# Weighing eight heads in one piece, with eight pairs of exponentials held, in the sixteen-head attentions of a fused kernel

## The chip, the cores and the metric

The kernel runs on one core of one Trainium2 chip. The metric is the device time in microseconds of one execution; three runs of the kernel before gave a median of 2002.47 us (1995.29 to 2004.57).

## The reference, cut to what matters

The program is a chain of twelve sub-layers on a residual of 8 x 256 tokens by 128 features. Two of its kinds are attentions with sixteen heads of width 8: the causal one (`_L1_attn_ref`, once) and the two-expert one (inside `_L3_ffn_ref`, used twice; its two experts double the number of heads).

```python
# L1, causal, 8 batches of 256 tokens, 16 heads of 8
scores = jnp.einsum('bhqd,bhkd->bhqk', q, k) * scale
scores = jnp.where(causal, scores, jnp.finfo(scores.dtype).min)
attn = jax.nn.softmax(scores, axis=-1)
out = jnp.einsum('bhqk,bhkd->bhqd', attn, v)
...
# L3, not causal, m = 2 experts
scores = jnp.einsum('mbhtk,mbhsk->mbhts', q, kk) / jnp.sqrt(jnp.float32(KD))
attn = jax.nn.softmax(scores, axis=-1)
ctx = jnp.einsum('mbhts,mbhsk->mbthk', attn, v)
```

## The kernel before, in words

Both attentions are one class, `SmallHeads` (`L1Attend` and `L3Attend` derive from it). The work is cut into units: one unit is sixteen heads of one batch of 256 tokens. `L1Attend` has 8 units, `L3Attend` 16 (8 batches by 2 experts), and `L3Attend` runs twice in the program. The order of the work is written by hand: `steps()` counts steps s, sixteen to a unit (k is the unit, i the step in it), and each engine walks through the same steps and does what is due at each. There is no scheduler. The engines meet by semaphores, and each takes its instructions in order.

What TensorE (PE) does for a unit is spread over four units' worth of steps:

- Step (k, i): the scores of head i of unit k, two bf16 matmuls from 48 rows, into one of three PSUM banks (`score_bank`). A score waits until the reduction of three steps before has left its bank (`topped`). VectorE (DVE) takes the row maximum of each head (L1484 in L3; L1482, two instructions with a mask, in L1).
- i = 0: the projections of unit k+2 (`project`, 128x256 with w_L3m or w_L1a).
- i = 3: the split maxima of unit k-1 are turned (ident_b matmuls). They come from GpSimd (POOL, L1522 to L1528), which waits for the last maximum; ScalarE (ACT, L1437) copies them out, and a DMA puts them into the stacked operands as three more rows, so that the second pass has 51 rows.
- Each odd step: a pair of heads of the second pass (`pair_at`, LAG = 25 steps after the head's scores), now with the maximum subtracted, four bf16 matmuls, into two of three other banks (`shifted_bank`). A pair waits until the first exponential of the pair before it is done (`exped`, 2g - 1). ACT takes the two exponentials (L1455, 128x512 in L3, 128x384 in L1) and writes them into `self.pt[g % 4]`, four buffers of one pair each. In L1, POOL then clears the two diagonal blocks (L1515) and raises `selected`.
- A quad (`quad_at`): four heads are weighed with their values: fp32 matmuls of 128 rows by 18 columns, four side by side in the four column groups of the array, into bank 6. The order tool's rows write them as 18x256 x8 in L3 and 18x256 x4 with 18x128 x4 in L1. The quad waits for its four exponentials (in L1 for `selected`). Four quads make a unit. In L3 they fall on i = 14, 2, 6 and 10, in L1 on i = 0, 4, 8 and 12.
- With the fourth quad of a unit (i = 10 in L3, 12 in L1) ACT copies bank 6 (`raw`, L1461), waiting for `weighed`; it does so before it takes the next exponentials.
- i = 5: `raw` is turned (L1351); DVE takes the reciprocals (L1490) and scales (L1493), behind the maximum of head 5 in its queue. i = 7: the values of unit k (128x128 with wv), for which PE waits for `scaled`, since both use bank 7. ACT copies them (L2237 in L3, L1667 in L1). i = 9: the context is turned back (L1365), ACT copies it with the bias (L2242, L1671). i = 11: the output product (w_L3m or w_L1a, 128x256), in L3 only in every second unit.

`S.activation(self.pt[g % 4]...)` is L1455, the quads' matmuls are at L1409, but all of PE's products go through the helper `mm`, so the profile shows them at L195. The shapes tell them apart: 48*128 is a score, 51*128 a pair, 128*18 a quad. In a PE row of the trace such neighbours are merged under the first one's shape.

Of the kernel before, what the change touches and what calls it, by code (L numbers as in the profile page):

```python
# [10 lines left out]
ACT = mybir.ActivationFunctionType  # L11
AXX = mybir.AxisListType.X

P = 128
# [5 lines left out]
BANK = 512  # L20
# [4 lines left out]
DEPTH, L0_HEADS, L0_DIM, WINDOW = 2, 8, 64, 64  # L25
# [1180 lines left out]
class SmallHeads(Stage):  # L1206
# [11 lines left out]
    def __init__(self, k, name, group, tag, members, causal):  # L1218
        super().__init__(k, name)
        a = self.arena  # L1220
        self.group, self.tag, self.members, self.units, self.causal = group, tag, members, BATCH * members, causal
        self.h = a.take(TOKENS)
        self.whole = [a.take(TOKENS) for _ in range(self.STACKS)]
        self.buffer2 = self.whole[2:4]
        self.stacks = [t.bitcast(BF16).rearrange("p (x g s) -> p x g s", x=2, g=self.PAIRS) for t in self.whole]
        self.q, self.kk = [t[:, 0] for t in self.stacks], [t[:, 1] for t in self.stacks]
        self.qk = [a.take(2 * SEQ).rearrange("p (x s) -> p x s", x=2) for _ in range(2)]
        self.rest = a.take(2 * SEQ).rearrange("p (x s) -> p x s", x=2)
        self.parts = a.take_bf16(2 * PARTS * SEQ).rearrange("p (a s) -> p a s", a=2 * PARTS)
        self.masked = a.take_bf16(3 * 3 * P).rearrange("p (e s) -> p e s", e=3)  # L1230
        self.va = [a.take(2 * HEADS * 3 * (KD + 1)).rearrange("p (n d) -> p n d", n=2 * HEADS) for _ in range(3)]
        self.mx = [a.take(2 * HEADS).rearrange("p (t h) -> p t h", t=2) for _ in range(2)]
        self.mx_rest = a.take(2 * HEADS).rearrange("p (x g) -> p x g", x=4)
        self.mx_parts = [a.take_bf16(2 * PARTS * HEADS).rearrange("p (x a g) -> p x a g", x=4, a=PARTS) for _ in range(2)]
        self.mx_rows = [a.take_bf16(SEQ, PARTS * HEADS) for _ in range(2)]
        self.pt = [a.take(2 * BANK).rearrange("p (h c) -> p h c", h=2) for _ in range(4)]
        self.raw = a.take(BANK)
        self.rinv = a.take(2 * HEADS).rearrange("p (a j) -> p a j", j=2)
        self.ctx = a.take(2 * P)
        self.ctxT = [a.take(SEQ) for _ in range(2)]  # L1240
        self.scale = float(1.0 / np.sqrt(np.float32(KD)))
        self.n1 = P if causal else SEQ
        U, H = self.units, HEADS
        self.cleared, self.opened = self.sig("cleared", 1), self.sig("opened", 1)
        self.projected, self.biased, self.low = (self.sig(n, U) for n in ("projected", "biased", "low"))
        self.valued, self.v_copied = self.sig("valued", U), self.sig("v_copied", U)
        self.scored, self.topped = self.sig("scored", H * U), self.sig("topped", H * U)
        self.mx_split, self.mx_turned, self.mx_copied = (self.sig(n, U) for n in ("mx_split", "mx_turned", "mx_copied"))
        self.shifted, self.exped, self.selected = self.sig("shifted", H * U), self.sig("exped", H * U), self.sig("selected", self.PAIRS * U)
        self.weighed = self.sig("weighed", self.QUADS * U)  # L1250
        self.raw_copied, self.turned, self.scaled, self.turned_again, self.ctx_copied = (
            self.sig(n, U) for n in ("raw_copied", "turned", "scaled", "turned_again", "ctx_copied"))
        self.summed, self.added = self.sig("summed", BATCH), self.sig("added", BATCH)
        self.loads = 2 * len(RUNS)
        turns = [(U + self.STACKS - 1 - i) // self.STACKS for i in range(self.STACKS)]
        self.parts_out = [self.sig(f"parts_out{i}", 16 * n) for i, n in enumerate(turns)]
        self.stacked = [self.sig(f"stacked{i}", 16 * self.loads * n) for i, n in enumerate(turns)]
        self.mx_stacked = [self.sig(f"mx_stacked{i}", 32 * n) for i, n in enumerate(turns)]
# [8 lines left out]
        g = (s - self.LAG) // 2  # L1267
        return g if s % 2 and 0 <= g < self.PAIRS * self.units else None

    def quad_at(self, s):  # L1270

        s -= self.LAG + (7 if self.causal else 5)
        w = s // 4
        return w if s % 4 == 0 and 0 <= w < self.QUADS * self.units else None

    def norm_at(self, s, steps):

# [43 lines left out]
    def heads_tensor(self, eng):  # L1321
        k_, ps, mm, T, U = self.k, self.k.ps, self.k.mm, self.k.nc.tensor, self.units
        for s, k, i in self.steps():
# [58 lines left out]
            if g is not None:  # L1382
# [6 lines left out]
                for t, (st, cnt, at) in enumerate(((0, SEQ, 0), (SEQ - self.n1, self.n1, SEQ))):  # L1389
                    for e in range(2):  # L1390
                        rows = slice(64 * e, 64 * e + self.ROWS + PARTS)
                        o = mm(ps[:, self.shifted_bank(2 * g + e), at:at + cnt], kk[rows, x, t * P:(t + 1) * P], q[rows, x, st:st + cnt])
                        if t:
                            o.then_inc(self.shifted.sem, 1)
            w = self.quad_at(s)
            if w is not None:
                u, x = w // self.QUADS, w % self.QUADS
                self.wait_ge(eng, *((self.selected, 2 * w + 2) if self.causal else (self.exped, 4 * w + 4)))
                if w == 0:
                    self.wait_ge(eng, self.opened, 1)  # L1400
                if x == 0:
                    self.wait_ge(eng, self.v_copied, u + 1)
                    self.wait_ge(eng, self.raw_copied, u)
                c, j = x // 2, x % 2
                for t, (st, cnt, at) in enumerate(((0, SEQ, 0), (SEQ - self.n1, self.n1, SEQ))):
                    for f in range(4):
                        h = 4 * x + f
                        v = self.va[u % 3][:, t * HEADS + h, (KD + 1) * (1 - j):(KD + 1) * (3 - j)]
                        o = mm(ps[32 * f:32 * f + 2 * (KD + 1), 6, c * SEQ + st:c * SEQ + st + cnt], v,  # L1409
                               self.pt[(2 * w + f // 2) % 4][:, f % 2, at:at + cnt], start=j == 0 and t == 0, stop=j == 1 and t == 1)  # L1410
                o.then_inc(self.weighed.sem, 1)
            c = self.norm_at(s, self.NORM_CENTERS)
            if c is not None:
# [9 lines left out]
    def heads_scalar(self, eng):  # L1423
        k_, ps, S = self.k, self.k.ps, self.k.nc.scalar
        for s, k, i in self.steps():
# [23 lines left out]
            g = self.pair_at(s)  # L1449
            if g is not None:  # L1450
                both = SEQ + self.n1
                self.wait_ge(eng, self.weighed, (g - 4) // 2 + 1)
                for e in range(2):
                    self.wait_ge(eng, self.shifted, 2 * g + e + 1)
                    S.activation(self.pt[g % 4][:, e, 0:both], ps[:, self.shifted_bank(2 * g + e), 0:both], ACT.Exp, scale=self.scale).then_inc(self.exped.sem, 1)  # L1455
            w = self.quad_at(s)
            if w is not None and w % self.QUADS == self.QUADS - 1:
                u = w // self.QUADS
                self.wait_ge(eng, self.weighed, w + 1)
                self.wait_ge(eng, self.turned, u)  # L1460
                S.activation(self.raw, ps[:, 6, :], ACT.Copy).then_inc(self.raw_copied.sem, 1)  # L1461
# [46 lines left out]
    def heads_gpsimd(self, eng, ch):  # L1508
        G, U = self.k.nc.gpsimd, self.units
        for s, k, i in self.steps():  # L1510
            g = self.pair_at(s)
            if self.causal and g is not None:
                pt = self.pt[g % 4][:, :, 0:3 * P].rearrange("p h (b c) -> p h b c", b=3)[:, :, 0:3:2]
                self.wait_ge(eng, self.exped, 2 * g + 2)
                G.affine_select(pt, pt, [[0, 2], [0, 2], [1, P]], ALU.is_ge, 0.0, base=0, channel_multiplier=-1).then_inc(self.selected.sem, 1)  # L1515
            u = k - 1
# [1136 lines left out]
```

## Time and profile before

| | |
|---|---|
| median of 3 runs | 2002.47 us (1995.29 to 2004.57) |
| span of the profiled execution (the page gives no other time of it) | 2003.0 us |
| TensorE busy | 84% |
| VectorE busy | 65% |
| ScalarE busy | 58% |
| GpSimd busy | 29% |
| the chain that ended last | PE 62%, DVE 13%, ACT 11%, issue 7%, POOL 4%, DMA 2% |
| causal attention (L1), from its first to its last score's maximum | 997.0 to 1099.7 us |
| the two L3 attentions, first to last maximum | 1354.9 to 1924.2 us, with experts and a scan between them |

The span is the time from the first to the last instruction of the profiled execution. Busy shares are means over the whole program, whose stages have different limits, so they don't say what bounds the attentions. A PE row of the timeline gives the start of a group, its length up to the modelled end of its last matmul, and in brackets what ended the idle time ahead of it. In the chain of waits each piece is the work that the next one waited for.

### The profile page before, as it was taken

What the parts mean: (1) busy time and instruction counts of PE and PEld (TensorE: products, weight loads), DVE (VectorE), ACT (ScalarE), POOL (GpSimd) and SP (SyncE); (2) the same over time, 40 slices, a digit from 0 to 9 for tenths busy, and PEclk for the clock granted to TensorE, in tenths of its full rate; (3) what the DMA queues carried; (4) which work ended last, traced back from release to release, by engine and by line L of the source; (5) the groups of instructions that cost most, each with busy time, mean ns of one, the idle gap of its engine ahead of it and who ended that gap; (6) DMA issues with size and microseconds to landing.
All of it is one profiled execution on the core that took longest, in us unless ns stands there. A gap on an engine that the chain in (4) does not pass through costs nothing.

```text
span 2003.0 us, 36848 instructions
## 1 busy us (share of the span) xinstructions
PE 1685.2 (84%) x13664; PEld 884.9 (44%) x13664; DVE 1299.4 (65%) x2611; ACT 1153.5 (58%) x2711; POOL 579.3 (29%) x727
## 2 busy tenths in 40 slices
PE   6897889798898889889688884978999877899986
PEld 2555345543455435553244332324555352355535
DVE  4875577545776577744577277637788464788856
ACT  3665455544455546555356664564888735488872
POOL 2552145301554045410265103313232001333200
PEclk9999999999899999989879897996999988699997
DMA  4000000000000000000252000015544000544401
GB/s 183 17 18 7 1 17 17 12 1 1 17 12 17 1 11 18 17 1 0 46 105 52 1 1 0 0 25 101 101 94 85 17 28 16 109 97 91 94 3 63
DMA packets 55016, 75.01 MB, mean 37 GB/s; under 512 B 5748, under 2 KB 38740, under 8 KB 54328
## 3 DMA queue, kind: packets, MB, share of 16 engines
q1 hardware_dynamic: 54840, 72.66, 16.0%
q8 instruction: 111, 1.82, 0.4%
q14 instruction: 65, 0.53, 0.1%
HBM read 46.39 MB, written 16.88 MB: 32 GB/s over the span
## 4 chain that ended last, share of the span: by engine, by line
PE 62%; DVE 13%; ACT 11%; issue 7%; POOL 4%; DMA 2%; SPq 0%; DVEq 0%; POOLq 0%; ACTq 0%
PE ps L195 58%; ACT arena L631 4%; DVE arena L1484 3%; PE ps L521 2%; ACT arena L1455 2%; DVE arena L702 2%; DVE arena L746 2%; ACT arena L268 1%; ACT arena L270 1%; PE ps L616 1%; PE ps L1365 1%; DVE arena L1493 1%; DMA arena<-arena 1%; DVE arena L721 1%; DMA arena<-scratch 1%
## 5 line engine op out<-in xcount | busy, mean ns | idle before, releaser
L195 PE MATMUL ps<-arena 32*64 32x128 f32 (+10 forms) x10152 | 705.0, 316 | 88.7 <-ACT arena L1455 25.5
L195 PEld LDWEIGHTS ps<-arena 32*64 32x64 f32 (+6 forms) x10152 | 397.7, 127 | 390.3 <-issue 124.5
L1455 ACT ACTIVATE arena<-ps 128x512 f32<-128x512 f32 (+1 forms) x640 | 333.8, 576 | 79.2 <-PE ps L195 70.4
L1484 DVE TENSOR_REDUCE arena<-ps 128x2 f32<-128x512 f32 x512 | 322.6, 685 | 87.2 <-PE ps L195 85.3
L195 PE MATMUL ps<-arena,w_L0f 128*128 128x512 f32 (+3 forms) x800 | 328.2, 542 | 16.9 <-DVEq L2488 9.3
L631 ACT ACTIVATE arena<-ps,arena 128x128 f32<-128x128 f32 x512 | 226.2, 460 | 136.0 <-DVE arena L748 136.0
L195 PE MATMUL ps<-arena,const 128*128 128x512 f32 (+1 forms) x536 | 186.1, 653 | 70.9 <-DVE arena L1966 22.1
L195 PEld LDWEIGHTS ps<-arena,w_L0f 128*128 128x128 f32 (+2 forms) x800 | 142.0, 192 | 142.4 <-issue 102.8
L828 POOL TENSOR_TENSOR arena<-arena 128x512 f32<-128x512 f32 x128 | 133.0, 1045 | 244.4 <-DVE arena L726 244.4
L702 DVE TENSOR_TENSOR arena<-ps,arena 128x1024 f32<-128x1024 f32 x128 | 152.4, 1205 | 10.0 <-PE ps L195 7.3
L642 ACT ACTIVATE arena<-ps 128x512 f32<-128x512 f32 x128 | 76.8, 600 | 94.4 <-DVE arena L702 91.7
L195 PEld LDWEIGHTS ps<-arena,const 128*128 128x128 f32 (+1 forms) x536 | 59.0, 161 | 158.2 <-issue 89.8
L820 POOL TENSOR_TENSOR arena<-arena 128x512 f32<-128x512 f32 x64 | 81.4, 1271 | 160.2 <-DVE arena L702 157.2
L746 DVE TENSOR_REDUCE arena<-ps 128x8 f32<-128x1024 f32 x64 | 78.3, 1223 | 63.7 <-PE ps L195 63.4
L721 DVE COPY arena<-ps 128x512 f32<-128x512 f32 x128 | 88.3, 689 | 47.7 <-PE ps L521 47.7
L631 ACT ACTIVATION_READ_ACCUMULATOR arena<-ps,arena 128x1 f32 x512 | 106.5, 208 | 0.0
L521 PE MATMUL ps<-const,arena 128*128 128x128 f32 x512 | 79.1, 277 | 30.2 <-issue 23.2
L1482 DVE CUSTOM_DVE_ANT_0 arena<-ps,masks_b 128x128 bf16<-128x128 f32 (+1 forms) x256 | 75.0, 354 | 36.2 <-PE ps L195 35.8
L521 PEld LDWEIGHTS ps<-const,arena 128*128 128x128 f32 x512 | 57.1, 141 | 93.2 <-issue 91.3
L1522 POOL CAST arena<-arena 128x32 bf16<-128x32 f32 x40 | 8.4, 209 | 280.0 <-DVE arena L1484 275.7
L821 POOL TENSOR_TENSOR arena<-arena 128x512 f32<-128x512 f32 x64 | 83.5, 1305 | 0.0
L195 PE MATMUL ps<-residual,const 128*128 128x512 f32 x96 | 56.9, 694 | 31.4 <-DVEq L2488 17.9
(227 smaller groups left out, 2134.2 us busy)
## 6 DMA issues: line engine op xcount, KB each, us to landing
scratch<-arena SPq DMA_DIRECT2D x40, 384.0 KB, 2.8
arena<-scratch SPq DMA_DIRECT2D x80, 192.0 KB
arena<-scratch SPq DMA_DIRECT2D x80, 128.0 KB
arena<-arena SPq DMA_DIRECT2D x64, 128.0 KB, 2.3
arena<-scratch SPq DMA_DIRECT2D x80, 88.0 KB
arena<-in_experts SPq DMA_DIRECT2D x16, 256.0 KB, 4.4
w_L0f<-in_L0f SPq DMA_DIRECT2D x2, 1557.0 KB, 12.2
arena<-arena SPq DMA_DIRECT2D x80, 12.0 KB
```

The source lines that it names most:

```text
L195: return self.nc.tensor.matmul(o, lhsT, rhs, start=start, stop=stop, skip_group_check=True)
L521: o = k.nc.tensor.transpose(k.ps[:, 6, (2 * j + t) * P:(2 * j + t + 1) * P], self.prob[G % 2][:, 2 * p + j, t, :], k.K("ident"))
L631: o = S.activation(self.prob[G % 2][:, j, t, :], k.ps[:, j, t * P:(t + 1) * P], ACT.Exp, bias=self.negm[G % 2][:, at:at + 1], scale=rn[:, ...
L642: self.k.nc.scalar.activation(self.sq[i], self.k.ps[:, self.block_bank(n), :], ACT.Square).then_inc(self.squared.sem, 1)
L702: self.k.nc.vector.tensor_tensor(prod.rearrange("p t (b s) -> p t b s", b=PER), x, tab, ALU.mult).then_inc(self.rotated.sem, 1)
L721: self.k.nc.vector.tensor_copy(self.probT[q % 4].rearrange("p j t s -> p (j t s)"), self.k.ps[:, 6, :]).then_inc(self.turn_copied.sem, 1)
L746: ch.did(V.tensor_reduce(self.mx[G % 2], ps[:, 0:4, 0:SEQ].rearrange("p j (t s) -> p j t s", t=2), AXX, ALU.max))
L820: G.tensor_tensor(y[:, i, :], first[:, 0, :], second[:, 1, :], ALU.add).then_inc(self.placed.sem, 1)
L821: G.tensor_tensor(y[:, i + 1, :], second[:, 0, :], first[:, 1, :], ALU.add).then_inc(self.placed.sem, 1)
L828: self.k.nc.gpsimd.tensor_tensor(pr, pr, rinv, ALU.mult).then_inc(self.scaled.sem, 1)
L1455: S.activation(self.pt[g % 4][:, e, 0:both], ps[:, self.shifted_bank(2 * g + e), 0:both], ACT.Exp, scale=self.scale).then_inc(self.exped.s ...
L1484: o = V.tensor_reduce(mx, ps[:, self.score_bank(s), :].rearrange("p (t s) -> p t s", t=2), AXX, ALU.max)
```

## The change

- Eight pairs of exponentials are held in place of four. The second four lie in the weights of the first sub-layer's local attention (`w_L0f0` and `w_L0f1`, two buffers of 1024 columns in each), which nobody reads any more when the attentions run. The index is `g % 8`, and ACT's wait for the quad that last read the buffer moves from four pairs back to eight.
- `quad_at` becomes `quads_at`: at every eighth step two quads are weighed one behind the other, in place of one at every fourth. In L3 they fall on i = 2 (quads 0 and 1) and i = 10 (quads 2 and 3), in L1 on i = 4 and i = 12. The second quad of each two keeps its step, the first comes four steps later than before. The copy of bank 6 stays at its step.
- Numbers of instructions, shapes and all other steps stay the same. The instructions of DVE and SP are in the same order as before.

```diff
-        self.pt = [a.take(2 * BANK).rearrange("p (h c) -> p h c", h=2) for _ in range(4)]
+        spent = [k.wt[f"L0f{l}"][:, x * 2 * BANK:(x + 1) * 2 * BANK] for l in range(DEPTH) for x in range(2)]
+        self.pt = [t.rearrange("p (h c) -> p h c", h=2) for t in [a.take(2 * BANK) for _ in range(4)] + spent]
...
-    def quad_at(self, s):
+    def quads_at(self, s):
 
-        s -= self.LAG + (7 if self.causal else 5)
+        s -= self.LAG + (11 if self.causal else 9)
         w = s // 4
-        return w if s % 4 == 0 and 0 <= w < self.QUADS * self.units else None
+        return (w, w + 1) if s % 8 == 0 and 0 <= w < self.QUADS * self.units else ()
...
-            w = self.quad_at(s)
-            if w is not None:
+            for w in self.quads_at(s):
...
                         o = mm(ps[32 * f:32 * f + 2 * (KD + 1), 6, c * SEQ + st:c * SEQ + st + cnt], v,
-                               self.pt[(2 * w + f // 2) % 4][:, f % 2, at:at + cnt], start=j == 0 and t == 0, stop=j == 1 and t == 1)
+                               self.pt[(2 * w + f // 2) % 8][:, f % 2, at:at + cnt], start=j == 0 and t == 0, stop=j == 1 and t == 1)
...
-                self.wait_ge(eng, self.weighed, (g - 4) // 2 + 1)
+                self.wait_ge(eng, self.weighed, (g - 8) // 2 + 1)
...
-                    S.activation(self.pt[g % 4][:, e, 0:both], ps[:, self.shifted_bank(2 * g + e), 0:both], ACT.Exp, scale=self.scale).then_inc(self.exped.sem, 1)
-            w = self.quad_at(s)
-            if w is not None and w % self.QUADS == self.QUADS - 1:
+                    S.activation(self.pt[g % 8][:, e, 0:both], ps[:, self.shifted_bank(2 * g + e), 0:both], ACT.Exp, scale=self.scale).then_inc(self.exped.sem, 1)
+            w = max(self.quads_at(s), default=0)
+            if w % self.QUADS == self.QUADS - 1:
...
-                pt = self.pt[g % 4][:, :, 0:3 * P].rearrange("p h (b c) -> p h b c", b=3)[:, :, 0:3:2]
+                pt = self.pt[g % 8][:, :, 0:3 * P].rearrange("p h (b c) -> p h b c", b=3)[:, :, 0:3:2]
```

PE in L3, from the pair and scores ahead of i = 14 to the quad of i = 10, before (18x256 is a quad, w_L3m 128x256 the projection of i = 0, ident_b i = 3, L1351 i = 5, w_L3m 128x128 i = 7, L1365 i = 9; 128x256 of the arena are scores and pairs):

```order
L195 MATMUL ps<-arena 18x256 x8
L195 MATMUL ps<-arena 128x256 x6
L195 MATMUL ps<-arena,w_L3m 128x256 x2
L195 MATMUL ps<-arena 128x256 x10
L195 MATMUL ps<-arena 18x256 x8
L195 MATMUL ps<-ident_b,arena 48x128 x2
L195 MATMUL ps<-arena 128x256 x8
L1351 MATMUL ps<-const,arena 128x128 x4
L195 MATMUL ps<-arena 128x256 x8
L195 MATMUL ps<-arena 18x256 x8
L195 MATMUL ps<-w_L3m,arena 128x128 x2
```

The same stretch of PE in the changed kernel:

```order
L195 MATMUL ps<-arena 128x256 x22
L195 MATMUL ps<-arena,w_L3m 128x256 x2
L195 MATMUL ps<-arena 128x256 x10
L195 MATMUL ps<-arena 18x256 x16
L195 MATMUL ps<-ident_b,arena 48x128 x2
L195 MATMUL ps<-arena 128x256 x8
L1352 MATMUL ps<-const,arena 128x128 x4
L195 MATMUL ps<-arena 128x256 x8
L195 MATMUL ps<-w_L3m,arena 128x128 x2
```

The quad of i = 14 has gone from between the scores to i = 2, and that of i = 6, between L1351 and the values, has gone to i = 10, outside the rows shown.

PE in L1 between i = 3 and i = 7 in the changed kernel, where one 18x256 x4 with its 18x128 x4 stood before:

```order
L195 MATMUL ps<-ident_b,arena 48x128 x2
L195 MATMUL ps<-arena 128x128
L195 MATMUL ps<-arena 128x256 x3
L195 MATMUL ps<-arena 128x128 x3
L195 MATMUL ps<-arena 128x256
L195 MATMUL ps<-arena 18x256 x4
L195 MATMUL ps<-arena 18x128 x4
L195 MATMUL ps<-arena 18x256 x4
L195 MATMUL ps<-arena 18x128 x4
L1352 MATMUL ps<-const,arena 128x128 x4
```

Quad 0, that stood at i = 0, now runs here ahead of quad 1 and of the turning of `raw` (L1352).

## Rows read from the trace of the kernel before

**Rows 1.** Stages by windows: us, busy time (instructions) by engine, PEclk, DMA share
```profile
1400.00:1500.00 100.00, 93.23 (x1083) 50.49 (x1079) 80.70 (x138) 81.53 (x164) 32.44 (x58) 1.00 0.46 94
...
1030.00:1090.00 60.00, 48.45 (x675) 26.92 (x674) 48.23 (x313) 41.82 (x99) 38.41 (x70) 1.00 0.39 79
...
1090.00:1120.00 30.00, 25.61 (x240) 11.44 (x242) 9.16 (x50) 17.03 (x40) 11.05 (x20) 0.71 0.01 2
```

**Rows 2.** The chain of waits in L3, pair of i = 13 to the next
```profile
1447.77 5.51 PE ps L195 x63
...
1453.31 1.18 DVE arena L1484 x2
...
1456.06 1.23 PE ps L195 x12
...
1460.89 5.51 PE ps L195 x63
```

**Rows 3.** PE's timeline in L3, in narrow windows: start us, us, group
```profile
1461.43 0.63 PE L195 MATMUL ps<-arena 128*18 128x256 f32 x8
...
1462.09 0.62 PE L195 MATMUL ps<-arena 128*18 128x256 f32 x6
...
1462.96 1.13 PE L195 MATMUL ps<-arena,w_L3m 128*128 128x256 f32 x4
...
1465.77 0.29 PE L195 MATMUL ps<-ident_b,arena 128*48 128x128 bf16 x2
...
1469.18 0.68 PE L195 MATMUL ps<-w_L3m,arena 128*128 128x128 f32 x4 [0.33 <-DVE arena L1493]
...
1472.66 1.13 PE L195 MATMUL ps<-arena,w_L3m 128*128 128x256 f32 x4
...
1474.98 0.28 PE L195 MATMUL ps<-arena 51*128 51x256 bf16 x2 [0.43 <-ACT arena L1455]
```

**Rows 4.** PE's weight loads in L3, the first behind a quad
```profile
1462.42 0.12 PEld L195 LDWEIGHTS ps<-arena 48*128 48x128 bf16 x4 [0.42 <-issue]
```

**Rows 5.** ACT's timeline in L3: the first exponential of i = 13
```profile
1461.38 0.60 ACT L1455 ACTIVATE arena<-ps 128x512 f32<-128x512 f32 x1
```

**Rows 6.** DVE's timeline in L3 around the scaling
```profile
1464.45 3.87 DVE L1484 TENSOR_REDUCE arena<-ps 128x2 f32<-128x512 f32 x6 [0.91 <-PE ps L195]
...
1468.61 0.42 DVE L1493 TENSOR_TENSOR arena<-ps,arena 128x256 f32<-128x256 f32 x1
```

**Rows 7.** The chain of waits in L3's tail
```profile
1583.80 1.09 ACT arena L1455 x2
...
1586.41 1.09 ACT arena L1455 x2
```

**Rows 8.** The chain of waits in L1, one unit
```profile
1052.15 1.90 PE ps L195 x26
...
1054.98 1.15 PE ps L195 x9
...
1057.46 0.88 ACT arena L1455 x2
...
1058.39 0.64 POOL arena L1515
...
1061.15 1.60 PE ps L195 x25
...
1065.16 0.84 PE ps L195 x5
```

**Rows 9.** L1: a quad on PE, and the first weight load behind it
```profile
1056.05 0.62 PE L195 MATMUL ps<-arena 128*18 128x256 f32 x7
...
1056.83 0.28 PEld L195 LDWEIGHTS ps<-arena 48*128 48x128 bf16 x8 [0.21 <-DVE arena L1482]
```

**Rows 10.** ACT's timeline in L1: exponentials of i = 7, copy of the context
```profile
1053.32 0.87 ACT L1455 ACTIVATE arena<-ps 128x384 f32<-128x384 f32 x2
...
1054.46 0.47 ACT L1671 ACTIVATE arena<-ps,cols 128x256 f32<-128x256 f32 x1 [0.26 <-PE ps L1365]
```

## The prediction

> **What bounds the kernel now.** I looked first at the stages, since only the three sixteen-head attentions can change. In the steady part of L3 (the second L3 attention reads the same) PE is busy for 93 of 100 us at a granted clock of 1.00, DVE and ACT for 81 each; in L1 PE and DVE have 48 of 60 us each, POOL 38 [rows 1]. A busy PE is a modelled figure, so the chain of waits decides. In L3 it repeats exactly [rows 2]. From the pair of i = 13 (1447.77, next 1460.89) PE itself is the chain for 5.51 us. Then DVE, with the maxima of heads 3 to 5 and the scaling, is the chain from 1453.31 until PE starts the values of i = 7 at 1456.06. From there it is PE again, up to the pair of i = 11, whose exponential on ACT releases the next pair of i = 13. The unit shown is one without an output product and takes 1460.89 - 1447.77 = 13.12 us. The next, with one, takes 1474.98 - 1460.89 = 14.09 us [rows 3]. The mean is 13.6 us.
>
> That difference of 0.97 us is the most useful number here: it is what one more block of work on PE behind the quad of i = 10 costs, and it is about what the product takes there (1472.66 to the next group, four passes of 0.22 us and a change of shape). Work added on PE at i = 10 or 11 therefore goes into the time one for one.
>
> **What a quad costs.** In L3 a quad is 16 matmul records, four side by side, so four waves. The first starts at 1461.43, the last at 1462.09 [rows 3], which makes 0.22 us from wave to wave. The next group's weights load at 1462.42 [rows 4]. From last wave to next group are 0.33 us, 0.11 more than a wave: the price of leaving this shape. No row prices the entering by itself; between nothing and the same again I take the same, about 0.10 for each change. The second of two quads behind each other thus adds 4 x 0.216 = 0.87 us and no change.
>
> **The change in a steady L3 unit, place by place.**
>
> 1. i = 10 gets quad 2 in addition: +0.87 us, one for one, as the output product shows. ACT can't help: it waits there for the end of both quads to copy bank 6.
> 2. i = 2 gets quad 0 in addition: +0.87 us. It lies in the stretch from 1460.89 to i = 3 at 1465.77 that is PE's own [rows 2, 3].
> 3. i = 14 loses its quad. PE's stretch from the pair of i = 13 (1460.89) to the projection (1462.96) is 2.07 us now [rows 3]. Without the quad PE comes to the pair of i = 15 after some 0.7 us, but this pair waits for the first exponential of i = 13: it starts on ACT at 1461.38 and takes 0.60 [rows 5], and PE goes on some 0.05 later, 1.15 us after 1460.89. The pair itself and the change of shape take 0.31 to the projection, so the stretch becomes 1.46 us: -0.61, not the whole 1.07 of a quad with its two changes. This wait is new and takes the quad's place.
> 4. i = 6 loses its quad: 0. Its 0.87 us lie under the DVE chain: from i = 3 (1465.77) to the values (1469.18) are 3.41 us, of which PE only needs the first two thirds. PE waits for L1493, which runs from 1468.61 to 1469.03 and stands behind the maximum of head 5 [rows 3, 6]. With the quad gone PE just waits about 1 us longer. The three maxima can't start earlier either, since head 3 comes from PE behind i = 3.
>
> The sum is 0.87 + 0.87 - 0.61 + 0 = **+1.13 us per unit**, 8% of 13.6. Two cheap blocks under cover are exchanged for two on the chain. DVE starves longer at i = 2, which costs nothing more, since PE's own time up to i = 3 is already counted.
>
> The 8 buffers by themselves cost and gain nothing. The old wait of ACT (a quad three steps back) always lay behind a pair that PE issues after that quad, so it was never last. The quads wait for exponentials of three steps ago as before. Where the buffers lie changes no instruction. The DMAs keep their place, and SP's order is the same.
>
> Of a stage's 16 units, 14 are steady (k = 2 to 15): +15.8 us. At k = 1 the quad of i = 14 goes away alone: -0.6. In the tail (k = 16, 17) pairs run without scores, at 2.61 us per four steps [rows 7], 1.09 of it the exponentials of a pair. With two quads between two pairs that gap becomes 2.15 us and the other three stay near 1.2, together 5.8 in place of 5.2 for eight steps: three times +0.55 = +1.6. An L3 stage has +16.8, both **+33.6 us**.
>
> **L1.** A unit takes 1065.16 - 1052.15 = 13.01 us. The chain [rows 8] goes from the values (1052.15) over PE to the output product (1054.98), the quad of i = 12, the copy of bank 6 and the exponentials of i = 13 and 15 (1057.46), two clearings on POOL (from 1058.39), the splitting of the maxima, i = 3 on PE (1061.15), the turning of `raw` and DVE's scaling to the next values. A quad is shorter: 1056.05 to 1056.83 with both changes [rows 9], 0.65 for a second one behind the first.
>
> - i = 8 loses its quad: the copy of the context, that started at 1054.46, then only waits for the exponentials of i = 7, which end at 1053.32 + 0.87 = 1054.19 [rows 10]: -0.27.
> - i = 12 gains one: +0.65. Up to i = 3 together +0.38: ACT's copy, the exponentials and both clearings are late by that much.
> - i = 0 loses its quad: 0, PE waits for POOL at i = 3 anyway.
> - i = 4 gains one, ahead of the turning of `raw`: +0.65.
>
> That is **+1.03 us per unit**, for six steady units +6.2. In the tail the granted clock is 0.71 in the mean [rows 1], so part of it at the lower level of 1.2 GHz, where a quad takes twice as long; I put +1.5 for it. L1 together: **+7.7 us**.
>
> **The sum**: 33.6 + 7.7 = +41.3 us on the profiled execution's span of 2003.0, which is the median (2002.47) to within 0.6 us. Forecast: **2044 us**, slower by 2.1%.
>
> **A rule that speaks for the change.** Each leaving of the 18-column shape shows as 0.11 us on PE [rows 3, 4]. The Trainium skill, "TensorEngine Tiling (Array Packing)", section "Key Properties", states that changing the tiling mode, not just the tile, drains the engine. By that rule alone, fewer changes of mode are fewer drains, and the kernel gets faster. The trace agrees that a change costs something, but the sum of the chain is not the sum of the drains.
>
> **The rivals.**
>
> - **Fewer changes of shape decide (faster).** If PE's own work bound every step, only the changes would count. A unit has three fewer: two around i = 14, and one of the three around i = 6, as the values still need their own. For 40 units, 3 x 0.10 x 40 = 12 us less: 1991 us. It would decide if PE's waits at i = 7 and i = 15 were not there. For it speaks PE's 93%. Against it: DVE's rows stand in the chain in every unit, and PE shows an idle time released by L1493 [rows 2, 3, 6]. Chance 0.07.
> - **The slack takes it all.** DVE and ACT are at 81%, so in principle 19% of a unit could absorb two longer blocks, and the deeper buffers could let them run ahead. Time 1999 to 2008. Against it: the three score banks and three pair banks are what limits running ahead, not the held exponentials, and the output product's 0.97 us are not absorbed either. Chance 0.05.
> - **Half of it.** If the pair of i = 15 isn't held up and i = 14 gives back its whole 1.07 us, a unit costs 0.87 + 0.87 - 1.07 = +0.67; with L1 at half its sum and no tail, 28 x 0.67 + 3 = +22: 2025 us. Chance 0.15.
> - **The clock goes too.** PE would idle some 1.5 us longer at a stretch in each unit, and where it had less to do around L1's tail the granted clock fell (0.71) [rows 1]. L1's steady part has 48 of 60 us busy and keeps 1.00, which speaks against it. If a tenth of the 540 us of attentions ran at 1.2 GHz, with PE on two thirds of the chain, that is some 25 us on top: 2069. Chance 0.08.
> - **The forecast**: 0.65.
>
> **The numbers.** The range goes from the half case to a starved case in which the double quads also make ACT late by another 0.3 us per unit (+12): 2021 to 2057. What lies outside are the faster and the unchanged case and most of the clock case, less than 2 in 10. A measurement of this kernel can tell about 0.5% (10 us) from no change. Slower by more than that: 0.88; within it, the slack case and the weak half of the first rival, 0.07; faster, 0.05.
>
> **What would show it.** If I am right, in L3 the unit with a product takes 15.2 us and the one without 14.25 in the chain; PE waits over 1 us for L1493 at i = 7; the pair of i = 15 is released by L1455 1.15 us behind the pair of i = 13; two quads take 1.73 us plus their changes, and the steady busy share of PE falls from 93% to about 87%. DVE idles about 1 us between heads 2 and 3. In L1 the unit takes about 14.0 us. I am wrong if the unit stays at 13.6 or less, if the values of i = 7 start earlier behind i = 3 than 3.4 us (then the scaling wasn't last there), or if PE shows other shapes' gaps shrinking.

## The result, and the profile after

The changed kernel takes 2074.31 us (median of 4 runs, 2069.11 to 2085.4) against 2000.11 for the kernel before. The ratio of the runs is 1.0367, with a 95% interval of 1.0329 to 1.0405: slower by 74 us, where the forecast said 41 and the range ended at 2057. The profiled execution has a span of 2083.7 us, 80.7 more than that of before; it is the slowest of the four, so the differences read from its trace are some 10 us larger than those of the medians.

First the chain of waits of one L3 unit without an output product, from values to values (start us, us, what):

```profile
1420.94 1.23 PE ps L195 x12
...
1422.71 3.20 PE ps L195 x47
...
1426.56 0.44 PE ps L195 x4
...
1427.05 0.61 ACT arena L1455
...
1427.70 4.62 PE ps L195 x55
...
1432.35 1.18 DVE arena L1484 x2
...
1433.55 0.68 DVE arena L1484
...
1435.10 1.23 PE ps L195 x12
```

The unit takes 1435.10 - 1420.94 = 14.16 us, where the forecast said 14.25; its counterpart in [rows 2] took 13.12, which was the longest of its kind: the other full units without a product in that trace take 13.04 or 13.05, so 13.04 + 1.13 = 14.17 was the figure to expect. The pair of i = 15 (1427.70) comes 1.14 us behind that of i = 13 (1426.56) and is released by the exponential in between (forecast 1.15). DVE is still the chain from head 3 to the scaling. PE's timeline of the same unit shows the wait that grew (start us, us, group, idle time ahead of it and its releaser):

```profile
1426.56 0.89 PE L195 MATMUL ps<-arena 51*128 51x256 bf16 x8 [0.45 <-ACT arena L1455]
1427.70 0.39 PE L195 MATMUL ps<-arena 51*128 51x256 bf16 x4 [0.25 <-ACT arena L1455]
...
1431.69 0.29 PE L195 MATMUL ps<-ident_b,arena 128*48 128x128 bf16 x2
...
1435.10 0.68 PE L195 MATMUL ps<-w_L3m,arena 128*128 128x128 f32 x4 [1.31 <-DVE arena L1493]
```

From i = 3 to the values are 3.41 us, as before [rows 3]; PE's wait there went from 0.33 to 1.31 us. A clean unit with an output product takes 15.20 us (forecast 15.2). Up to here the working holds. The rest is in the windows: us, busy time by engine, then the granted clock (PEclk). Two consecutive units, and the same stages as [rows 1]:

```profile
1420.94:1435.10 14.16, 12.02 (x144) 6.67 (x145) 10.63 (x19) 10.95 (x22) 4.46 (x8) 1.00 0.46 92
1435.10:1451.93 16.83, 14.66 (x149) 7.77 (x149) 11.07 (x20) 11.05 (x22) 4.39 (x8) 0.90 0.40 73
```
```profile
1400.00:1500.00 100.00, 86.45 (x934) 46.01 (x932) 68.45 (x118) 70.65 (x142) 31.08 (x56) 0.92 0.41 80
1800.00:1900.00 100.00, 86.80 (x926) 47.06 (x930) 69.37 (x119) 70.91 (x142) 28.14 (x54) 0.91 0.42 82
1030.00:1090.00 60.00, 48.04 (x562) 27.03 (x562) 38.95 (x254) 34.47 (x81) 33.24 (x59) 0.83 0.39 79
```

The second unit should take 15.20 and takes 16.83: part of it ran at the lower of the two clock levels (1.2 GHz), which makes a mean of 0.90, and costs 1.63 us. "Low stretch" below means such a time at the lower level. The two L3 attentions together have 24 intervals from one scaling to the next in which scores are still made. Before, none of them had a granted clock under 1.00, and neither had L1's first four; now 16 of the 24 have, and all four of L1's. PE's busy time per 100 us of L3 is 86.5, as forecast (87), though some of it is work at half speed; the clean unit above has 12.02 of 14.16 us, 85%.

By stages, in the profiled execution of each kernel (each stage from its first scaling to its last; in brackets the part of it at the lower clock level, us):

| run | L1 | both L3 attentions | all the rest |
|---|---|---|---|
| kernel before | 89.4 (23.9) | 383.8 (0) | 1529.9 |
| single_eight | 84.3 (6.8) | 383.6 (0) | 1528.2 |
| changed kernel | 104.7 (44.4) | 444.9 (71.7) | 1534.1 |
| fill_gap | 90.7 (6.8) | 421.0 (10.2) | 1532.6 |
| fill_other | 94.6 (17.1) | 454.7 (64.9) | 1530.5 |
| pair_first | 91.9 (17.1) | 398.2 (13.7) | 1533.5 |
| pair_second | 99.2 (41.0) | 427.6 (54.6) | 1527.7 |
| long_wait | 102.2 (51.2) | 407.0 (51.2) | 1528.7 |
| less_two | 84.2 (6.8) | 373.8 (17.1) | 1526.2 |
| less_two_warm | 85.6 (10.2) | 371.2 (10.2) | 1522.2 |

The 89.4 us of L1 in the kernel before are unusual: single_eight, less_work, less_at_10, less_two, less_all and less_two_warm leave L1's instructions as they were and have 84.2 to 86.9. What differs is the tail, where the trace that the forecast was read from had more of the lower clock than the others.

### The profile page after: what moved, and what is told of

Its sections match the earlier page's. It is cut to its first block, busy times and chain, and to the rows that moved or that the text cites. A ratio compares the mean times of both kernels' runs of the same rounds, so it can differ in the third digit from the quotient of the medians.

```text
span 2083.7 us, 36836 instructions
## 1 busy us (share of the span) xinstructions
PE 1727.2 (83%) x13664; PEld 908.3 (44%) x13664; DVE 1298.1 (62%) x2611; ACT 1154.3 (55%) x2711; POOL 579.7 (28%) x727
## 4 chain that ended last, share of the span: by engine, by line
PE 63%; DVE 14%; ACT 11%; issue 7%; POOL 3%; DMA 2%; SPq 0%; DVEq 0%; POOLq 0%; ACTq 0%
PE ps L195 58%; ACT arena L631 4%; DVE arena L1484 3%; PE ps L521 2%; ACT arena L1455 2%; DVE arena L702 2%; DVE arena L746 1%; ACT arena L268 1%; ACT arena L270 1%; PE ps L616 1%; PE ps L1366 1%; DVE arena L721 1%; DMA arena<-arena 1%; DMA arena<-scratch 1%; DVE arena L1493 1%
## 5 line engine op out<-in xcount | busy, mean ns | idle before, releaser
L195 PE MATMUL ps<-arena 32*64 32x128 f32 (+10 forms) x8872 | 647.1, 314 | 100.7 <-ACT arena L1455 27.6
L195 PEld LDWEIGHTS ps<-arena 32*64 32x64 f32 (+6 forms) x8872 | 378.0, 132 | 376.5 <-issue 133.1
L195 PE MATMUL ps<-arena,const 128*128 128x512 f32 (+1 forms) x536 | 191.6, 672 | 68.9 <-DVE arena L1966 22.1
L828 POOL TENSOR_TENSOR arena<-arena 128x512 f32<-128x512 f32 x128 | 133.2, 1047 | 240.9 <-DVE arena L726 240.9
L1455 ACT ACTIVATE arena<-ps 128x512 f32<-128x512 f32 (+1 forms) x320 | 167.1, 576 | 35.5 <-PE ps L195 30.7
L1455 ACT ACTIVATE w_L0f<-ps 128x512 f32<-128x512 f32 (+1 forms) x320 | 166.8, 574 | 35.3 <-PE ps L195 28.7
L195 PE MATMUL ps<-w_L0f,arena 128*18 128x256 f32 (+2 forms) x1408 | 168.9, 476 | 0.0
L820 POOL TENSOR_TENSOR arena<-arena 128x512 f32<-128x512 f32 x64 | 81.4, 1272 | 162.4 <-DVE arena L702 159.5
L521 PEld LDWEIGHTS ps<-const,arena 128*128 128x128 f32 x512 | 57.1, 141 | 92.7 <-issue 90.7
## 6 DMA issues: line engine op xcount, KB each, us to landing
w_L0f<-in_L0f SPq DMA_DIRECT2D x2, 1557.0 KB, 12.3
```

The source lines that it names most:

```text
L195: return self.nc.tensor.matmul(o, lhsT, rhs, start=start, stop=stop, skip_group_check=True)
L521: o = k.nc.tensor.transpose(k.ps[:, 6, (2 * j + t) * P:(2 * j + t + 1) * P], self.prob[G % 2][:, 2 * p + j, t, :], k.K("ident"))
L820: G.tensor_tensor(y[:, i, :], first[:, 0, :], second[:, 1, :], ALU.add).then_inc(self.placed.sem, 1)
L828: self.k.nc.gpsimd.tensor_tensor(pr, pr, rinv, ALU.mult).then_inc(self.scaled.sem, 1)
L1455: S.activation(self.pt[g % 8][:, e, 0:both], ps[:, self.shifted_bank(2 * g + e), 0:both], ACT.Exp, scale=self.scale).then_inc(self.exped.s ...
```

## The experiments

The runs are described below. Full-clock unit times are the distance from one scaling to the next in units whose granted clock is 1.00 throughout, without and with an output product. PEclk is the granted clock of 1400 to 1560 us, which lies inside the first L3 attention in each kernel. It says nothing of the second L3 attention or of L1. The kernel before has 13.04 and 14.09 us and 1.00. Each ratio is taken against the kernel before run beside it, whose median was 1996.94 to 2003.18 us, so a few us between medians of different runs mean nothing.

| run | median us | ratio (95%) | L3 unit at full clock | PE's wait at i = 7 | PEclk |
|---|---|---|---|---|---|
| changed kernel | 2074.31 | 1.037 (1.033 to 1.041) | 14.16 / 15.20 | 1.31 | 0.90 |
| single_eight | 1996.67 | 0.998 (0.995 to 1.001) | 13.04 / 14.08 | 0.33 | 1.00 |
| fill_gap | 2045.16 | 1.022 (1.016 to 1.027) | 14.16 / 15.20 | 0.33 | 0.99 |
| fill_other | 2087.73 | 1.047 (1.042 to 1.051) | 14.77 / 15.81 | 1.31 | 0.95 |
| pair_first | 2022.40 | 1.010 (1.004 to 1.016) | 13.29 / 14.34 | 0.33 | 0.99 |
| pair_second | 2054.81 | 1.026 (1.019 to 1.032) | 13.91 / 14.95 | 1.32 | 0.91 |
| pairs_shifted | 2043.58 | 1.023 (1.018 to 1.028) | 13.59 / 14.28 | none | 0.97 |
| less_work | 1997.36 | 1.001 (0.999 to 1.003) | 13.04 / 14.09 | 0.98 | 0.99 |
| long_wait | 2046.01 | 1.023 (1.019 to 1.028) | 13.27 / 14.30 | 1.31 | 0.96 |
| less_at_10 | 2004.97 | 1.002 (1.000 to 1.005) | 12.97 / 13.43 | 0.33 | 0.94 |
| less_all | 2024.63 | 1.012 (1.005 to 1.019) | 12.17 / 12.64 | 1.17 | 0.78 |
| less_two | 1994.95 | 0.998 (0.996 to 1.001) | 12.78 / 13.25 | 0.54 | 0.98 |
| less_two_warm | 1981.93 | 0.991 (0.987 to 0.994) | 12.78 / 13.25 | 0.55 | 0.98 |

### single_eight: the buffers alone

```diff
     def quads_at(self, s):
-        s -= self.LAG + (11 if self.causal else 9)
+        s -= self.LAG + (7 if self.causal else 5)
         w = s // 4
-        return (w, w + 1) if s % 8 == 0 and 0 <= w < self.QUADS * self.units else ()
+        return (w,) if s % 4 == 0 and 0 <= w < self.QUADS * self.units else ()
```

> The changed kernel with its eight buffers, but with single quads at their old steps. Both theories (the places of the quads cost the time, with or without the clock) expect the time of before, 2000 us within 0.3%, and L3 units of 13.04 and 14.09 us. If the buffers or their place in the spent weights cost something, the time stays above 2010.

0.998: no difference, and the same units as before. Eight buffers, four of them in the spent weights, cost and gain nothing. All of the 74 us come from where the quads stand.

### fill_gap and fill_other: the same added work at two places

```diff
+            for w in self.filler_at(s):
...
+                        mm(ps[32 * f:32 * f + 2 * (KD + 1), 6, c * SEQ + st:c * SEQ + st + cnt], v,
+                           self.pt[(2 * w + f // 2) % 8][:, f % 2, at:at + cnt], start=t == 0, stop=t == 1)
             for w in self.quads_at(s):
```

`filler_at` (cut here) gives quad 2 in L3 (i = 6) and quad 0 in L1 (i = 0), at the steps of before. The real quads overwrite what the filler writes.

> The changed kernel with its double quads, and one more quad in addition whose result is thrown away (bank 6 is overwritten by the real one): in L3 at i = 6, where PE otherwise waits 1.3 us for the scaling, in L1 at i = 0, where it waits for POOL. Clock theory: the low granted clock in the changed kernel comes from these waits of PE; with them filled the clock stays at 1.00 in the steady part, the added work is free, L3 units take 14.2 and 15.2 us each, and the whole takes 2040 to 2045 us, some 30 us less than without the added work. Rival (the double blocks, or something else about the new order, lower the clock or delay the engines): the time stays at 2074 or rises by the added work.

The kernel with the work of a quad more per unit takes 29 us less than without it: 2045.16. PE's timeline of fill_gap in L3, from the double quad of i = 10 to the values:

```profile
1448.59 1.92 PE L195 MATMUL ps<-w_L0f,arena 128*18 128x256 f32 x32
1450.44 1.13 PE L195 MATMUL ps<-arena,w_L3m 128*128 128x256 f32 x4
...
1459.92 1.06 PE L195 MATMUL ps<-w_L0f,arena 128*18 128x256 f32 x16
1461.30 0.68 PE L195 MATMUL ps<-w_L3m,arena 128*128 128x128 f32 x4 [0.33 <-DVE arena L1514]
```

The releaser, L1514 in this kernel's numbering, is the same scaling (L1493 before). The wait is back at 0.33 us, the added quad (1459.92) lies fully under it, and the units at full clock are unchanged, 14.16 and 15.20. So the work was free and what it brought is the clock:

```profile
1400.00:1560.00 160.00, 146.78 (x1744) 79.78 (x1746) 117.79 (x202) 119.35 (x238) 46.06 (x85) 0.99 0.44 88
```

for which the changed kernel has

```profile
1400.00:1560.00 160.00, 139.17 (x1472) 74.00 (x1474) 108.19 (x185) 111.57 (x224) 45.43 (x85) 0.90 0.41 82
```

fill_gap also has both double quads, so these don't lower the clock by themselves. Its profiled span is 2044.3 us, 41.3 more than before. That this is just the sum of the forecast is in part luck: against single_eight, whose L1 tail is the usual one, the L3 attentions take 37.4 us more (forecast 33.6; three low stretches are in it), L1 6.5 (forecast 7.7) and the rest of the program 4.4 (forecast 0).

> As fill_gap, with the same quad's worth of added work in L3, but at i = 14, where PE has only some 0.4 us of waiting, in place of i = 6; the wait of 1.3 us at i = 7 stays. If that long wait is what lowers the clock: low stretches stay in the steady L3 units and the work added on the chain (about 0.6 us a unit) comes on top: 2075 to 2100 us. If the clock only goes by how much PE does in a unit (rival): no low stretches, units of 14.8 and 15.9 us, 2062 us.

fill_other puts its L3 filler at quad 0's old step, i = 14, with everything else the same. The units at full clock grow by 0.61 as forecast (14.77 and 15.81), the low clock stays, and the time is 2087.73. PE's wait at i = 7 is the changed kernel's:

```profile
1441.12 0.68 PE L195 MATMUL ps<-w_L3m,arena 128*128 128x128 f32 x4 [1.31 <-DVE arena L1514]
```

The same amount of added work brings 29 us at one place and costs 13 at another. In 1400 to 1560 us the clock is better than in the changed kernel (0.95 against 0.90), but over both L3 attentions it is nearly the same: 64.9 us at the lower level, against 71.7 there and 10.2 in fill_gap. So the place decides, and that the amount counts too isn't shown. L1 has the filler at i = 0 in both runs, and in both it is shorter than in the changed kernel (90.7 and 94.6 against 104.7 us).

### pair_first and pair_second: one double quad each

```diff
     def quads_at(self, s):
-        s -= self.LAG + (11 if self.causal else 9)
+        s -= self.LAG + (7 if self.causal else 5)
         w = s // 4
-        return (w, w + 1) if s % 8 == 0 and 0 <= w < self.QUADS * self.units else ()
+        if s % 4 or not 0 <= w < self.QUADS * self.units:
+            return ()
+        x = w % self.QUADS
+        return {1: (w - 1, w), 2: (w,), 3: (w,)}.get(x, ())
```

(pair_second has `{0: (w,), 1: (w,), 3: (w - 1, w)}`.)

> Only quads 0 and 1 of each unit are weighed together (i = 2 in L3, i = 4 in L1); quads 2 and 3 keep their steps. By the chain of waits a steady L3 unit costs 0.87 - 0.61 = +0.26 us and an L1 unit +0.65: 7 + 4 = +11 us, 2011. Clock theory: the wait for the scaling at i = 7 stays at 0.3 to 0.4 us, so no steady L3 unit shows a low granted clock, and 2011 is all. Rival (double blocks or the new wait at i = 15 lower the clock): low stretches in steady L3 units, at 1.6 us each, 2020 or more.

> Only quads 2 and 3 are weighed together (i = 10 in L3, i = 12 in L1); quads 0 and 1 keep their steps. By the chain alone a steady L3 unit costs +0.87 us, an L1 unit +0.4: 24 + 2 = 2027 us. Clock theory: PE's wait at i = 7 grows to 1.3 us as in the changed kernel, steady L3 units show low stretches, and the time is 2045 to 2060. Rival (it isn't that wait): 2027 and a clock of 1.00 in the steady units.

The chain's terms come out to 0.01 us: pair_first has 13.29 and 14.34, +0.25 (forecast +0.26); pair_second 13.91 and 14.95, +0.87 (forecast +0.87). The sum of both is the changed kernel's +1.12. In L3 the clock falls widely only with the second (0.91 against 0.99), the one that empties i = 6. The totals are higher than the chain's: pair_first is at 2022, not 2011, and so where the expectation had put the rival. Two low stretches at the end of each L3 attention cost about 3 us there, 6 in both. L1 takes 7.6 us more than in single_eight, where some 4 were expected, and has 17.1 us at the lower level against 6.8. In pair_second L1 has 41.0 us at the lower level, although its quad at i = 0 keeps its place: there i = 8 is emptied.

### less_work and long_wait: the wait without the double quads

less_work is the kernel before with quad 2 of L3 multiplied from truncated operands:

```diff
                         v = self.va[u % 3][:, t * HEADS + h, (KD + 1) * (1 - j):(KD + 1) * (3 - j)]
+                        pt = self.pt[(2 * w + f // 2) % 4][:, f % 2, at:at + cnt]
+                        if x == 2 and not self.causal:
+                            v, pt = v.bitcast(BF16)[:, 1::2], pt.bitcast(BF16)[:, 1::2]
...
```

long_wait is pair_second with the same three lines.

> The kernel before, with one thing less for PE: in L3, quad 2 (i = 6, under the scaling) is multiplied from the upper halves of its fp32 operands, read as bf16, so heads 8 to 11 are weighed with truncated numbers. That takes about 0.65 us of PE's work out of every L3 unit, at the one place that the chain of waits doesn't use; PE's wait at i = 7 grows from 0.33 to about 1 us. Clock theory: some steady L3 units get a low granted clock, at 1.6 us each, and the kernel becomes slower though it does less: 2005 to 2030 us. Chain alone (rival): L3 units stay at 13.04 and 14.09 us with a clock of 1.00, 2000 us.

> As pair_second (quads 2 and 3 together at i = 10 in L3, 12 in L1), with L3's quad 2 multiplied from the upper halves of its operands, read as bf16, as in less_work. PE has the same work in an L3 unit as in less_work, but its wait for the scaling at i = 7 is 1.3 us in place of 0.98, and the chain is some 0.2 to 0.3 us longer. If the length of the wait decides on the clock: low stretches in a third to a half of the steady L3 units, 2025 to 2040 us. If only the amount of PE's work counts (rival): steady L3 units as clean as in less_work, 13.3 and 14.4 us, and about 2018 us (of which some 12 are L1's, as in pair_second).

PE's wait in less_work and in long_wait:

```profile
1448.74 0.68 PE L195 MATMUL ps<-w_L3m,arena 128*128 128x128 f32 x4 [0.98 <-DVE arena L1495]
```
```profile
1446.51 0.68 PE L195 MATMUL ps<-w_L3m,arena 128*128 128x128 f32 x4 [1.31 <-DVE arena L1498]
```

less_work was a miss: with a wait of 0.98 us its steady L3 units are 13.04 and 14.09, one of the 24 intervals touched by the low clock, and the time is that of before. The other half of it is confirmed: 0.65 us of work out of i = 6 shortens the unit by nothing. long_wait, with the same work per L3 unit and a wait of 1.31 us, has low stretches in 11 of the 24 and takes 2046, 28 us more than the 2018 without low stretches in L3, and more than the 2025 to 2040 expected. In its trace the L3 attentions take 23 us more than in single_eight, of which the chain explains some 6, and L1 18 us more. Between the two kernels lie a third of a microsecond of waiting at i = 7 and quad 2 at i = 10 in place of i = 6, and in L1 a quad moved too. So the same work in an L3 unit can keep the clock or lose it. That the wait does it fits fill_gap, but these two runs don't separate it from the order around it, and there is no simple length: L1 before had a wait of 1.38 us in each unit and kept 1.00 [rows 1], as the trace of before shows at 1052.15:

```profile
1052.15 0.68 PE L195 MATMUL ps<-w_L1a,arena 128*128 128x128 f32 x4 [1.38 <-DVE arena L1493]
```

### pairs_shifted: both double quads under cover

```diff
-        s -= self.LAG + (11 if self.causal else 9)
+        s -= self.LAG + (15 if self.causal else 13)
```

> The changed kernel with both double quads four steps later: L3 at i = 6 and i = 14, L1 at i = 8 and i = 0. By the chain, L3's double quad at i = 6 is mostly under the scaling (+0.5 us, the half us that PE comes late to the values), i = 10 gives back 0.4 to 0.75, i = 14 takes 0.87 and i = 2 gives 0.95 back: a unit of 13.0 and 13.7 us, 13.4 in the mean against 13.6 before. L1: +0.35 at i = 0, -0.7 at i = 4, +0.65 at i = 8, -0.75 at i = 12: 12.5 us. The clock theory expects 1.00 in the steady L3 units, since PE doesn't wait at i = 7 any more. Together 1990 to 1995 us, a little faster than before. If double blocks hurt by themselves: slower than before, 2010 or more.

A miss. The units are 13.59 and 14.28 us, 0.6 more than I had worked out, and the end of each L3 attention is longer, since the last double quad waits at i = 14. Nor does the clock stay at 1.00, as the clock theory had it: though PE doesn't wait at i = 7 any more, 41 of 421 us in L3 are at the lower level, most of them at the end of each attention. The chain shows what I left out (start us, us, what):

```profile
1482.69 0.42 issue
1483.12 0.59 ACT w_L0f L1455
1483.71 0.37 ACT arena L2242
...
1484.12 1.69 PE ps L195 x11
1485.81 0.59 ACT arena L1455
```

The double quad at i = 6 makes the pair of i = 7 late, and through it ACT: its exponentials and the copy of the context (L2242) become the chain up to the output product.

### less_at_10, less_all, less_two, less_two_warm: less work, and the version that beats both

These are less_work's edit with other quads of L3: `x == 3`; all four; `x % 2` (quads 1 and 3). less_two_warm adds to less_two:

```diff
-                for t in range(2):
+                for t in (0, 0, 0, 1) if i == 13 and not self.causal and k >= 2 else (0, 1):
```

> The kernel before, with quad 3 of L3 (i = 10) in place of quad 2 multiplied from the upper halves of its operands, read as bf16: the same 0.65 us of work less for PE as in less_work, but at a place where I hold that work counts one for one. A unit with an output product should come down by 0.65 to 13.4 us; one without by about 0.3 to 12.7, since the pair of i = 11 then waits for an exponential. 28 steady units: 1983 to 1988 us. Rival (the sum of PE's work counts, not the place): as less_work, where the same saving gave nothing, 1997.

> The kernel before, with all quads of L3 multiplied from the upper halves of their operands, read as bf16 (all heads of L3 weighed with truncated numbers), in their old places. By the chain: i = 2 gives 0.65 us, i = 10 0.3 to 0.65, i = 14 the 0.4 us up to the wait for the exponential, i = 6 nothing: about 1.5 us a unit, 12.1 in the mean, 1958 us if the clock holds. PE is then idle for over 2 us a unit, among it 1 us at i = 7. Clock theory: low stretches come and take back part of it, 1965 to 1995 us.

> The kernel before, with quads 1 and 3 of L3 (i = 2 and i = 10, the two places on PE's own chain) multiplied from the upper halves of their operands, read as bf16 (heads 4 to 7 and 12 to 15 of L3 weighed with truncated numbers), and quads 0 and 2 (i = 14 and 6, which lie beside waits) left in fp32. Chain at full clock: i = 2 gives 0.65 us, i = 10 0.1 to 0.65: units of 12.3 and 12.8 us, 33 us less in 28 units. Clock theory: PE's busy stretches at i = 6 and 14 are kept, so there is less of the low clock than in less_all, but some, as in less_at_10: 1970 to 1995 us. It would be the first version faster than both kernels. If total work decides: as less_all, 2015 or more.

> As less_two, with added work for PE in L3: the first of the two products of head 13's score is issued three times (the same numbers into the same place), just ahead of PE's wait for the exponential at i = 13. The chain pays nothing in units without an output product and up to 0.2 us in the others. If more work beside the wait keeps the clock up: fewer low stretches than in less_two and some 5 to 10 us less. If two bf16 products more don't matter to the clock: the same as less_two within 3 us, or up to 4 us more.

At i = 10 the work counts where an output product follows (14.09 to 13.43, forecast 13.4), and hardly without one (12.97, forecast 12.7). In the chain of such a unit the exponential at i = 11 comes next. But steady units get the low clock, and the time, 2004.97, is not below that of before: a miss of 17 us. less_all, a miss too (1965 to 1995 expected), shows it at its plainest. Its window:

```profile
1400.00:1560.00 160.00, 141.47 (x1268) 74.46 (x1266) 121.24 (x206) 121.35 (x244) 45.21 (x84) 0.78 0.44 87
```

PE has 2.6 us of work less in each unit, a clean unit takes 12.17 or 12.64 us (12.4 in the mean, forecast 12.1), and the kernel is slower than before, 2024.63 against 2001.08, because half of L3 (208 of 411 us) runs at the low level. PE's waits in a unit of it:

```profile
1450.44 0.68 PE L195 MATMUL ps<-w_L3m,arena 128*128 128x128 f32 x4 [1.17 <-DVE arena L1495]
...
1455.27 1.53 PE L195 MATMUL ps<-arena 51*128 51x256 bf16 x20 [0.85 <-ACT arena L1457]
```

less_two keeps the covered quads in fp32. Its units are 12.78 and 13.25 us, not the 12.3 and 12.8 forecast: beside less_at_10 the work taken from i = 2 brings 0.2 us and not 0.65, as DVE's maxima become the chain there (in the chain of waits of less_two at i = 2 and 3; before they came in only at head 3):

```profile
1444.71 2.84 DVE arena L1486 x5
```

The clock is 0.98. Its ten runs spread from 1982.98 to 2007.70 (median 1994.95), so it can't be told from before. less_two_warm adds two products of head 13's score that change nothing just ahead of the wait at i = 13, which become part of that wait:

```profile
1454.07 2.14 PE L195 MATMUL ps<-arena 51*128 51x256 bf16 x28 [0.85 <-ACT arena L1457]
```
```profile
1447.33 2.14 PE L195 MATMUL ps<-arena 51*128 51x256 bf16 x28 [0.64 <-ACT arena L1457]
```

(first less_two, then less_two_warm). The units are the same to 0.01 us, and the time is 1981.93 (1974.61 to 1987.00): ratio 0.991, 0.987 to 0.994. It is faster than both kernels by about 1%, with products that nobody needs, and with heads 4 to 7 and 12 to 15 of L3 weighed with truncated numbers. Against less_two the medians are 13 us apart. The two profiled executions are only 5.2 us apart, half of it in the L3 attentions, with 10.2 us at the lower level against 17.1, and the window of the table has 0.98 in both. So the added products made it faster, but that they did so through the clock is shown only in small part.

## Why the prediction was wrong

**What held.** Every term of the chain of the forecast in L3 at full clock. One block at i = 10: +0.87, measured +0.87 alone. The two moves around i = 2 and i = 14: +0.26, measured +0.25. The quad of i = 6 under the scaling: 0, measured 0 by less_work and by fill_gap. The sum +1.13, measured +1.12. L1's block at i = 4 was +0.65 and measured 0.56 (13.57 against 13.01 in a clean unit of pair_first); clean L1 units of fill_gap take 13.8 to 14.2 against a forecast of 14.04. With most of the clock held, the whole was 2045.16 against a forecast of 2044, in part by luck, as said at fill_gap.

**What failed** is first of all the term of 0 at i = 6 in L3 ("i = 6 loses its quad: 0", with "PE just waits about 1 us longer"). On the chain of waits 0 is right. For the time it is not, because the forecast held the clock at 1.00. The quad at i = 6 was PE's work in its longest wait of the L3 unit. With the work put back there and at i = 0 in L1, 29 us come back (changed kernel against fill_gap); without it they stand on top of the chain's 41. L1's terms, too, were priced on the chain alone. The rival "The clock goes too" named this mechanism, at a chance of 0.08 and with its 2069 us outside the range. The reason given against it, that L1's steady part has 48 of 60 us busy and keeps 1.00, was no reason. PE's busy share doesn't decide it: the changed L3 is busy for 86 of 100 us, more than L1 was, and has 0.92. The rival's own size was low too, a tenth of the attentions at the lower level: in the changed kernel it is 116 of 550 us. Against fill_gap this is 99 us more, and the traces are 39 us apart: 24 in the two L3 attentions, 14 in L1 and 1 or 2 elsewhere. So a third of the loss is L1's, whose steady part went from 1.00 to 0.83, and one us at the lower level cost about 0.4 us in either.

The rival on fewer changes of shape wasn't borne out: the kernel got slower, and every term of the chain is matched without it. The slack rival and the half case fell with the +1.12. The tail's +1.5 us in L1 was worked out from a tail with more of the lower clock than the other kernels show, so no run confirms it.

**What stays open.** What it is that lowers the clock. Not the length of the longest wait alone (L1 before: 1.38 us at 1.00; less_work: 0.98 at 0.99; long_wait: 1.31 at 0.96; pairs_shifted: no wait at i = 7, at 0.97; less_at_10: 0.33 and a second wait at i = 13, at 0.94). Not the amount of work alone (fill_gap and fill_other). How the waits lie to each other within a unit seems to count, but no run here tells it apart. Which move in L1 costs its clock is open as well: emptying i = 8 (pair_second) brings more of the low level than emptying i = 0 (pair_first), 41.0 us against 17.1, and yet work put back at i = 0 takes most of it away (fill_gap, 6.8).

## What to carry to other kernels

Price a move of TensorE's work on the chain of waits, and then ask a second question of the place that it leaves: does this empty a wait that was filled? Work under a wait is free on the chain, but it can be what holds the granted clock, and then taking it away costs more than leaving it. Where a profile after a change shows PEclk falling in a stage that had 1.00, put cheap products back into the wait before you blame the order. Here this won back 29 of the 74 us, and the order of before is still the faster one. And a place on PE's own chain counts one for one only for added work: work taken away there counts until the next engine's chain takes over (0.2 of 0.65 us at i = 2).

## What the runs showed that I had not expected

- PE doing 2.6 us less in each L3 unit of 13.6 us made the kernel 24 us slower (less_all, granted clock 0.78 in L3), and added products made it faster twice: by 29 us in fill_gap, by 13 in less_two_warm against less_two.
- The step between a wait of 0.98 and one of 1.31 us at i = 7, with the same work in the unit: 1 interval of 24 with the low clock against 11 (quad 2 stands at another step, too).
- A hand-worked chain of one unit, from a single profile, was right to 0.1 us where work was added or moved (14.16, 13.29, 13.91, 14.77, and long_wait's 13.27). It was wrong by 0.6 in pairs_shifted, in which I did not follow ACT's queue, and by 0.3 to 0.5 where work was taken off PE's own chain (less_at_10 without a product, less_all, less_two).
